# Exponentials and value products of four full attentions as a list of their own, and keys and queries in column halves

## The chip, the cores and the metric

The kernel runs on one core of one Trainium2 chip. The metric is device microseconds of one execution. The kernel before took 2460.37 us (median of 3 runs, 2451.26 to 2460.69).

## What is computed

`x` is [2, 1024, 256] in float32: two batches (b = 0, 1) of 1024 tokens. Four blocks follow each other, all with 16 heads of 16 channels where they attend.

```python
x = _L0(x)   # adaLN, window self-attention (128), top-16 cross-attention, SwiGLU MLP
x = _L1(x)   # prototype attention, three routed experts, gate
x = _L2(x)   # adaLN, masked full self-attention with rotary positions, cross-attention, GELU MLP
x = _L3(x)   # adaLN, full self-attention, cross-attention, GELU MLP

# the part that the change is about, in _L2 (with a mask) and in _L3 (without)
s = einsum('bqhd,bkhd->bhqk', q, k) * scale      # 1024 x 1024 scores per head
s = where(mask, s, finfo.min)                    # _L2 only
a = softmax(s, axis=-1)
o = einsum('bhqk,bkhd->bqhd', a, v)
```

## The kernel before

Work is written as *stages* (a norm, the keys of a batch, an attention, an MLP). A stage has one generator for each engine (`tensor`, `vector`, `scalar`, `pool`, `sync`); each `yield` ends a *step*, and a step is usually one instruction or one group of matmuls. The stages stand in *lists*: list 0 mostly holds the attentions, list 1 (its lane is `lane_d`) holds what runs beside them, the norms, projections, cross-attentions, MLPs and experts; a third list has loads for SyncE alone. For each engine, a string in `ORDER` says in which order the steps of the lists are issued: its characters are run lengths, in turn for list 0, list 1 and so on. The strings were written by a planner, ahead of time. Each engine works through its merged steps in order and waits on semaphores where it must.

A full attention (`Attention` with kind "full") treats 8 groups of 2 heads. For one group:

- SyncE loads the group's queries and keys, split in three bf16 parts each, from DRAM into a stack (`load`, L1072 and L1158). The stage `Begin` does that ahead for the first groups; the other loads are in the attention's own SyncE steps. The second block's attentions have two stacks, the last block's have three. A stack comes free after the last exponential of the group that had it.
- `max_tile` (L1224): 32 tiles of scores, 128 queries x 512 keys, into the banks 0 and 1. `max_of` (L1375 with the mask, L1378 without) takes each tile's row maxima on VectorE.
- The rows' maxima are joined (L1347), turned (L1193), split into two bf16 parts (`rows`, L1332 and L1335) and stored by SyncE into two rows of the query stack (L1171), so that the next matmul subtracts them.
- `exp_tile` (L1253): 32 tiles of transposed scores, 128 keys x 512 queries, into the banks 2 and 3. In the second block the mask is added, for half of the tiles by four small matmuls (L1258), for the other half ahead of the scores by ScalarE (L1318, `write_mask`). ScalarE takes the exponentials (L1300).
- `pv` (L1282): for every four tiles, the value products, four strips at once into bank 4. At the end of a group the sums are copied by ScalarE (`finish_copy`, L1080), turned (`finish_turn`, L1087), and divided by VectorE (`finish_out`, L1098 and L1104).

All of this was one stage in list 0, in beats: the exponentials of a group follow its maxima by 40 beats, with a period of 40 beats (second block) or 32 (last block), so that the exponentials of group g run with the maxima of group g + 1, one tile of each in turn. In the first 40 beats of an attention there are maxima alone, and in the last ones exponentials alone.

Keys and queries are made by `Parts` in four steps each, two column halves (channels 0 to 127 and 128 to 255) by two token blocks: matmuls (L854), ScalarE copies (L871, L877), VectorE splits (L926 and following), and three stores to DRAM by SyncE per step (L951), 12 for the keys and 12 for the queries of a batch. `PartsOf` does one column half of a `Parts`. The columns of half 0 hold the heads of groups 0 to 3. The function `halves` was already used for the first block and for the second block's batch 0:

```python
def halves(b, keys, queries, *begin):
    k, q = S_[b][keys], S_[b][queries]
    return [PartsOf(k, 0), PartsOf(q, 0), PartsOf(k, 1), *begin, PartsOf(q, 1)]
```

For the other three, the phase has keys, then queries, then values (`Values`, L999, L1021), then `Begin`. After the attention's outputs come the output projection (L1725, L1753, additions on VectorE at L1647) and the next norm (statistics at L719 and L724, turns at L767).

## Time and profile before

| | |
|---|---|
| median of 3 runs | 2460.37 us (2451.26 to 2460.69) |
| the profiled execution, its own time | 2454.07 us |
| its span in the profile | 2452.8 us |
| TensorE, VectorE, ScalarE busy | 92%, 69%, 57% |
| the four full attentions | 858 to 2250 us |

A profile shows one execution. Matmuls are pipelined: a matmul counts as busy from its start to its modelled end, so the times of neighbours overlap, and the starts show how fast TensorE goes. PE is TensorE's matmul, PEld its weight load, DVE VectorE, ACT ScalarE, POOL GpSimd, SP SyncE.

### The profile page before, as it was taken

The page shows a single profiled execution, that of the slowest core. Times are in us where ns is not written, and L with a number is a line of the kernel's source. Part 1 is how long each engine was busy: PE and PEld are TensorE (multiplying, and loading weights), DVE is VectorE, ACT ScalarE, POOL GpSimd, SP SyncE. Part 2 cuts the span into 40 slices and gives each one's busy share as a digit, 9 for nine tenths or more (in the row PEclk, how much of TensorE's full clock was granted, in tenths as well). Part 3 has the DMA queues.
Part 4 walks back from the last instruction along what each step waited for, and adds up shares of the span by engine and source line. Part 5 has one row for each costly group of instructions (what it writes and reads, how often), then busy time and mean ns, then how long its engine had stood idle before and what let it go on. Part 6 is the DMA issues. An engine that isn't in the chain of part 4 may idle for free.

```text
span 2452.8 us, 35316 instructions
## 1 busy us (share of the span) xinstructions
PE 2264.3 (92%) x12135; PEld 1146.1 (47%) x12135; DVE 1681.0 (69%) x5149; ACT 1407.8 (57%) x2698; POOL 371.9 (15%) x409
## 2 busy tenths in 40 slices
PE   7988799989998989998989999988999989999987
PEld 3675355645655644433343445443435342334554
DVE  7667876864325765677877776758786778885553
ACT  3434445543233236777848887855676747776543
POOL 3013533342201100000100010000020010002022
PEclk8998999998998979999989999988999999999999
DMA  7666521000001310001222200133130132210220
GB/s 232 167 180 193 159 79 33 14 22 5 14 1 47 121 16 14 23 18 53 99 87 67 60 23 14 47 113 99 46 79 14 52 97 85 62 40 7 61 65 18
DMA packets 151080, 161.06 MB, mean 66 GB/s; under 512 B 33423, under 2 KB 120291, under 8 KB 150637
## 3 DMA queue, kind: packets, MB, share of 16 engines
q1 hardware_dynamic: 150900, 158.80, 22.5%
q8 instruction: 96, 1.57, 0.3%
q14 instruction: 84, 0.68, 0.1%
HBM read 97.39 MB, written 60.19 MB: 64 GB/s over the span
## 4 chain that ended last, share of the span: by engine, by line
PE 73%; DVE 14%; ACT 6%; DMA 3%; issue 2%; POOL 2%; SPq 1%; ACTq 0%; DVEq 0%; POOLq 0%
PE bank L1282 10%; PE bank L1253 9%; PE bank L1833 9%; PE bank L1224 8%; PE bank L1856 6%; PE bank L2378 4%; PE bank L854 4%; PE bank L2558 3%; DVE max L1378 2%; PE bank L1753 2%; PE bank L1258 2%; ACT work L1300 2%; PE bank L2380 2%; PE bank L767 2%; PE bank L1087 2%
## 5 line engine op out<-in xcount | busy, mean ns | idle before, releaser
L1300 ACT ACTIVATE work<-bank 128x512 f32<-128x512 f32 (+1 forms) x1216 | 685.7, 595 | 271.5 <-PE bank L1253 173.4
L1375 DVE CUSTOM_DVE_ANT_0 bank<-bank,weights 128x512 f32<-128x512 f32 x512 | 347.8, 706 | 122.5 <-PE bank L1224 120.6
L1224 PE MATMUL bank<-k_stack,q_stack 97*128 97x512 bf16 x896 | 354.4, 401 | 34.2 <-DVE max L1378 15.5
L1378 DVE TENSOR_REDUCE max<-bank 128x1 f32<-128x512 f32 x512 | 334.5, 684 | 58.9 <-PE bank L1224 56.9
L1253 PE MATMUL bank<-q_stack,k_stack 99*128 99x512 bf16 x896 | 339.3, 384 | 21.5 <-ACT bank L1318 17.0
L1833 PE MATMUL bank<-hT,weights 128*128 128x512 f32 x512 | 254.2, 612 | 7.5 <-ACT hT L811 4.1
L1224 PEld LDWEIGHTS bank<-k_stack,q_stack 97*128 97x128 bf16 x896 | 88.5, 99 | 287.5 <-DVE max L1378 109.0
L1856 PE MATMUL bank<-weights,work 128*128 128x256 f32 x768 | 195.0, 383 | 4.2 <-DVE work L1923 3.8
L1856 PEld LDWEIGHTS bank<-weights,work 128*128 128x128 f32 x768 | 141.2, 190 | 67.9 <-issue 28.9
L1253 PEld LDWEIGHTS bank<-q_stack,k_stack 99*128 99x128 bf16 x896 | 86.7, 98 | 172.4 <-ACT work L1300 78.9
L1318 ACT ACTIVATE bank<-weights 128x512 f32<-128x512 uint8 x256 | 153.9, 602 | 6.9
L854 PE MATMUL bank<-hT,weights 128*128 128x512 f32 x288 | 150.8, 632 | 3.6 <-ACT hT L811 3.5
L1365 DVE TENSOR_REDUCE max<-bank 128x4 f32<-128x308 f32 (+1 forms) x192 | 101.8, 544 | 54.3 <-PE bank L1230 53.3
L1282 PE MATMUL bank<-work,v 128*17 128x512 f32 x1024 | 134.8, 598 | 0.0
L1282 PE MATMUL bank<-work,weights 128*17 128x512 f32 x1024 | 134.8, 598 | 0.0
L1833 PEld LDWEIGHTS bank<-hT,weights 128*128 128x128 f32 x512 | 93.7, 194 | 87.0 <-issue 60.1
L2378 PE MATMUL bank<-hT,weights 128*128 128x512 f32 (+1 forms) x240 | 123.3, 624 | 0.4 <-ACT work L2576 0.3
L1625 POOL TENSOR_TENSOR x<-x,row_consts 128x256 f32<-128x256 f32 x112 | 86.2, 770 | 189.1 <-DMA row_consts<-in_L_b_cproj 174.4
L2572 ACT ACTIVATE work<-bank,half_anchor 128x512 f32<-128x512 f32 x56 | 38.4, 686 | 113.2 <-PE bank L2380 106.3
L1258 PEld LDWEIGHTS bank<-ident_b,weights 128*128 128x128 bf16 x1024 | 79.0, 97 | 48.1 <-issue 0.3
L767 PE MATMUL bank<-ident,work 128*128 128x128 f32 x320 | 70.5, 339 | 31.7 <-DVE work L745 29.5
L1258 PE MATMUL bank<-ident_b,weights 128*128 128x128 bf16 x1024 | 99.1, 218 | 0.0
(236 smaller groups left out, 3669.8 us busy)
## 6 DMA issues: line engine op xcount, KB each, us to landing
q_stack<-parts_q SPq DMA_DIRECT2D x60, 384.0 KB, 4.0
k_stack<-parts_k SPq DMA_DIRECT2D x40, 384.0 KB, 5.0
parts_q<-parts SPq DMA_DIRECT2D x38, 384.0 KB, 2.5
weights<-parts_q SPq DMA_DIRECT2D x36, 384.0 KB, 3.6
parts_q<-parts SPq DMA_DIRECT2D x38, 256.0 KB, 2.9
parts_k<-parts SPq DMA_DIRECT2D x24, 384.0 KB, 2.6
parts_k<-parts SPq DMA_DIRECT2D x24, 256.0 KB, 2.9
weights<-in_L_e_w SPq DMA_DIRECT2D x12, 512.0 KB, 5.9
```

What stands on the lines that cost most here:

```text
L854: m = pe.e.matmul(bank.ap[:, :], w[:, i, self.col + c * P:self.col + (c + 1) * P], hT[self.b][:, bl, i, :], start=i == 0, stop=i == CC - 1)
L1224: m = pe.e.matmul(bank.ap[:, :], self.q(g)[0:MAX_ROW, h, qt * P:(qt + 1) * P], k_stacks[self.key, g].ap[0:MAX_ROW, h, half * BLK:(half + 1 ...
L1253: m = pe.e.matmul(bank.ap[0:self.nk, :], self.k(g, h, STACK, kt * P), q, start=not written, stop=written or not self.mask, skip_group_chec ...
L1258: m = pe.e.matmul(bank.ap[:, j * P:(j + 1) * P], mask_bias[:, half * TPB + j, kt * P:(kt + 1) * P], ident_b[:, :], start=False, stop=j == ...
L1282: m = pe.e.matmul(o[strip:strip + DV, :], self.v[:, kt, head, :] if self.own else self.v[:, head, :], p[0:self.nk, :], start=kt == 0, stop ...
L1300: ac.e.activation(p.ap[0:self.nk, :], banks[self.key, "exp", g, i].ap[0:self.nk, :], ACT.Exp).then_inc(*probs.tick((self.key, g, i)))
L1318: ac.e.activation(bank.ap[:, :], masked_of[self.b][:, i // 4, :], ACT.Copy, scale=MASKED).then_inc(*evac.tick((self.key, "masked", g, i)))
L1375: ve.e.tensor_tensor_reduce(bank[:, :], bank[:, :], mask_bias[:, qt, half * BLK:(half + 1) * BLK], 1.0, -3.4e38, ALU.add, ALU.max, to).the ...
L1378: ve.e.tensor_reduce(to, bank[:, :], AX_X, ALU.max).then_inc(*maxima.tick((self.key, g, i)))
L1833: m = pe.e.matmul(banks[key].ap[:, :], w1[:, k, col:col + P], hT[self.b][:, bl, k, :], start=k == 0, stop=k == CC - 1)
L1856: m = pe.e.matmul(banks[self.key, tp].ap[:, i * C:(i + 1) * C], hid[:, at * P:(at + 1) * P], w2[:, j, :], start=(j == 0 and i == 0), stop= ...
L2378: return pe.e.matmul(out, wt[name][:, k, lo:hi], hT[self.b][:, self.bl, k, :], start=k == 0, stop=False)
```

## The change

1. `Attention` of kind "full" becomes `FullAttention`, whose steps on TensorE and VectorE are the maxima and what belongs to them; on ScalarE it has none. A new stage `Weighting` has the exponentials, masks written by ScalarE, value products, and the finish of a group. The four `Weighting` stages stand in a list of their own. The beats without an instruction are no longer steps.
2. The merge of TensorE, VectorE and ScalarE goes over three lists.
3. Keys and queries of the second block's batch 1 and of the last block's both batches are made by `halves`, with `Begin` for one group (before: two, two and three groups, behind the values).
4. All order strings are new, over the whole kernel.

```diff
@@ ORDER: every string of the five engines is replaced; the first line of two of them
     "tensor": (
-        "1932342d1e3a912142328142c45222c222h2c132l142f2o2222e315bb343724341Mal2c272636432227212927273eb56526961ea622442234181"
+        "1903202403r0490910220420720430420220a20540120d20610d10310g10j20h20na0860580960630330650610Oa0h10510c2021021071022024"
     "scalar": (
-        "0Zdi6b629hb714221B521bl6bZakd755272696DbUk2126948321835451Zl5kfa4b8b838i7113898o8gg1171c112a12c3bc4a24172529le757a63"
...
@@ Attention.scalar
-                        g, i = now
-                        p = work[self.key, "prob", g, i]
...
+                        yield from self.exponentials(ac, *now)
+            def exponentials(self, ac, g, i):
+                p = work[self.key, "prob", g, i]
+                if self.mask and (g, i) == (0, 0):
+                    for first in range(2):
+                        self.write_mask(ac, 0, first)
+                        yield
+                for f in p.free:
+                    ac.wait_ge(*f)
+                ac.wait_ge(*exp_scores[self.key, g, i])
+                ac.e.activation(p.ap[0:self.nk, :], banks[self.key, "exp", g, i].ap[0:self.nk, :], ACT.Exp).then_inc(
+                    *probs.tick((self.key, g, i)))
+                yield
...
@@ new stages
+        class FullAttention(Attention):
+            def tensor(self, pe):
+                turns = 0
+                for beat in range(self.beats):
+                    if now := self.group(beat, 0, self.n):
+                        self.max_tile(pe, *now, turns)
+                        yield
+                        turns += 1
+                    if now := self.group(beat, self.rows_at + 1, 1):
...
+                        pe.e.transpose(bank.ap[0:PAIR * NT, 0:P], max1[self.key, g].ap[:, :], ident[:, :]).then_inc(
+                            *turned.tick((self.key, "rows", g)))
+                        yield
+                        turns += 1
+            def scalar(self, ac):
+                return iter(())
+            def vector(self, ve):
+                for beat in range(self.beats):
+                    if now := self.group(beat, self.rows_at + 2, 1):
+                        yield from self.rows_of(ve, now[0])
+                    if now := self.group(beat, 0, self.n):
+                        self.max_of(ve, *now)
+                        yield
+                    if now := self.group(beat, self.rows_at, 1):
+                        self.both_halves(ve, now[0])
+                        yield
+        class Weighting(Stage):
+            def __init__(self, attn):
+                self.attn = attn
+            def tensor(self, pe):
+                attn = self.attn
+                for beat in range(attn.beats):
+                    if now := attn.group(beat, attn.exp_at, attn.n):
+                        attn.exp_tile(pe, *now)
+                        yield
+                    if now := attn.group(beat, attn.pv_at, attn.n):
+                        if now[1] % 4 == 0:
+                            attn.pv(pe, now[0], now[1] // 4)
+                            yield
+                    if now := attn.group(beat, attn.fin_at + attn.late, 1):
+                        g = now[0]
+                        bank = banks.take(attn.bank("pv", g), (attn.key, "turn", g), (vec, (attn.key, "out", g)))
+                        attn.finish_turn(pe, g, bank)
+                        yield
+            def scalar(self, ac):
+                attn = self.attn
+                for beat in range(attn.beats):
+                    if now := attn.group(beat, attn.exp_at, attn.n):
+                        yield from attn.exponentials(ac, *now)
+                    if now := attn.group(beat, attn.fin_at, 1):
+                        attn.finish_copy(ac, now[0])
+                        yield
+            def vector(self, ve):
+                attn = self.attn
+                for g in range(attn.groups):
+                    yield from attn.finish_out(ve, g)
@@ build_program
-            st["self2"] = Attention(lane_a, b, "L2", "full", ...
+            st["self2"] = FullAttention(lane_a, b, "L2", "full", ...
-            st["self3"] = Attention(lane_a, b, "L3", "full", ...
+            st["self3"] = FullAttention(lane_a, b, "L3", "full", ...
-        begin_win1, begin_self1 = Begin(two_["win"]), Begin(two_["self2"])
-        begin_last, begin_last1 = Begin(one_["self3"], 2), Begin(two_["self3"])
+        begin_win1, begin_self1 = Begin(two_["win"]), Begin(two_["self2"], 1)
+        begin_last, begin_last1 = Begin(one_["self3"], 1), Begin(two_["self3"], 1)
-            (of(0, "self2"), of(1, ("e", 1, "n"), ("e", 1)) + [v_high2, mask_copy] + of(1, "n4", "k2", "q2", "v2") + [early(0, "so2"), begin_self1],
-             [Rest(30), load_l2m, load_l3]),
+            (of(0, "self2"), of(1, ("e", 1, "n"), ("e", 1)) + [v_high2, mask_copy] + of(1, "n4") + halves(1, "k2", "q2", begin_self1) + of(1, "v2") + [early(0, "so2")],
+             [Rest(30), load_l2m, load_l3], [Weighting(one_["self2"])]),
...
-             + of(0, "mlp2", "n7", "k3", "q3") + [early(0, "v3")] + of(0, "v3") + [early(1, "so2"), begin_last]),
+             + of(0, "mlp2", "n7") + halves(0, "k3", "q3", begin_last) + [early(0, "v3")] + of(0, "v3") + [early(1, "so2")], [], [Weighting(two_["self2"])]),
...
-            merge(ORDER["tensor"], *[itertools.chain.from_iterable(s.tensor(pe) for s in lane) for lane in lanes[0:2]])
+            merge(ORDER["tensor"], *[itertools.chain.from_iterable(s.tensor(pe) for s in lane) for lane in (lanes[0], lanes[1], lanes[3])])
```

The turn of a finished group now takes the bank of the value products (4) in place of one of the two maxima banks.

## Rows read from the trace of the kernel before

**Rows 1.** The page: its span, and busy time of each engine.
```profile
span 2452.8 us, 35316 instructions
...
PE 2264.3 (92%) x12135; PEld 1146.1 (47%) x12135; DVE 1681.0 (69%) x5149; ACT 1407.8 (57%) x2698; POOL 371.9 (15%) x409
```

**Rows 2.** The page's costliest groups: busy us, mean ns, idle before.
```profile
L1300 ACT ACTIVATE work<-bank 128x512 f32<-128x512 f32 (+1 forms) x1216 | 685.7, 595 | 271.5 <-PE bank L1253 173.4
L1375 DVE CUSTOM_DVE_ANT_0 bank<-bank,weights 128x512 f32<-128x512 f32 x512 | 347.8, 706 | 122.5 <-PE bank L1224 120.6
L1224 PE MATMUL bank<-k_stack,q_stack 97*128 97x512 bf16 x896 | 354.4, 401 | 34.2 <-DVE max L1378 15.5
L1378 DVE TENSOR_REDUCE max<-bank 128x1 f32<-128x512 f32 x512 | 334.5, 684 | 58.9 <-PE bank L1224 56.9
L1253 PE MATMUL bank<-q_stack,k_stack 99*128 99x512 bf16 x896 | 339.3, 384 | 21.5 <-ACT bank L1318 17.0
...
L1318 ACT ACTIVATE bank<-weights 128x512 f32<-128x512 uint8 x256 | 153.9, 602 | 6.9
```

**Rows 3.** Timeline of TensorE in the last attention: start us, duration us.
```profile
2131.11 0.39 PE L1224 MATMUL bank<-weights 97*128 97x512 bf16 x1
2131.33 0.38 PE L1253 MATMUL bank<-q_stack,k_stack 99*128 99x512 bf16 x1
```

**Rows 4.** Busy time by stage: length, each engine's busy us, granted clock, DMA.
```profile
0.00:858.00 858.00, 766.05 (x3882) 472.46 (x3883) 557.61 (x2414) 345.56 (x809) 238.47 (x264) 0.94 0.31 90
...
908.00:1230.00 322.00, 303.70 (x1802) 130.23 (x1800) 224.17 (x617) 247.39 (x431) 17.47 (x13) 1.00 0.14 41
1230.00:1272.00 42.00, 33.42 (x142) 18.18 (x140) 30.71 (x94) 12.45 (x23) 5.08 (x5) 0.84 0.24 62
1272.00:1618.00 346.00, 336.96 (x2132) 154.99 (x2132) 245.02 (x694) 287.02 (x512) 17.31 (x18) 1.00 0.20 58
1618.00:1682.00 64.00, 52.40 (x185) 23.81 (x185) 49.47 (x101) 19.38 (x34) 6.02 (x6) 0.76 0.32 96
1682.00:1978.00 296.00, 292.59 (x1579) 122.28 (x1579) 218.07 (x455) 206.82 (x377) 22.07 (x25) 1.00 0.22 59
1978.00:2020.00 42.00, 34.68 (x146) 19.17 (x145) 36.80 (x82) 11.62 (x21) 9.72 (x12) 0.92 0.21 55
2020.00:2250.00 230.00, 224.95 (x1349) 76.05 (x1347) 183.59 (x370) 170.07 (x315) 12.88 (x17) 1.00 0.18 52
```

**Rows 5.** Timeline of TensorE where the second attention begins.
```profile
1234.92 1.03 PE L999 MATMUL bank<-weights,hT 128*128 128x256 f32 x4
1238.07 0.59 PE L1224 MATMUL bank<-k_stack,q_stack 97*128 97x512 bf16 x2 [2.12 <-DMA k_stack<-parts_k]
...
1252.14 0.60 PE L1224 MATMUL bank<-k_stack,q_stack 97*128 97x512 bf16 x2
1257.17 1.26 PE L1224 MATMUL bank<-k_stack,q_stack 97*128 97x512 bf16 x2 [4.44 <-DVE max L1375]
```

**Rows 6.** Timeline of VectorE in that pause.
```profile
1252.94 0.75 DVE L719 BATCH_NORM_STATS2 stats<-x 128x6 f32<-128x256 f32 x2
...
1255.53 0.72 DVE L719 BATCH_NORM_STATS2 stats<-x 128x6 f32<-128x256 f32 x2
```

**Rows 7.** Timeline of SyncE's DMA issues ahead of the second attention.
```profile
1216.29 13.05 SPq L951 DMA_DIRECT2D parts_q<-parts  x9
...
1230.59 0.49 SPq L1158 DMA_DIRECT2D k_stack<-parts_k  x1
```

**Rows 8.** What weight loads waited for, 858 to 2250 us: total, times, longest.
```profile
PEld bank L1224 <- DVE max L1378: 135.7, 242, 4.7
PEld bank L1224 <- DVE max L1375: 105.7, 152, 4.9
PEld bank L1253 <- ACT work L1300: 90.6, 192, 1.0
...
PEld bank L1253 <- ACT bank L1318: 55.7, 101, 1.0
```

**Rows 9.** Timeline of TensorE where the fourth attention begins.
```profile
1984.42 0.59 PE L1224 MATMUL bank<-k_stack,q_stack 97*128 97x512 bf16 x2 [0.50 <-DMA k_stack<-parts_k]
```

More of the change, by code:

```diff
@@ L1309, in scalar @@
                         yield
+                    yield
[11 more added lines that the diff above has]
+                yield
+                n = g * self.n + i + 2
+                if self.mask and n < self.groups * self.n and self.head_half(n % self.n)[1] == 0:
+                    self.write_mask(ac, n // self.n, n % self.n)
                     yield
@@ L1339, in vector, with rows_of, both_halves @@
                         yield
[L1340 to L1350 removed]
+                    yield
+            def rows_of(self, ve, g):
+                mp = max_parts.take(self.in_a, (self.key, g), (ld_m[self.q_lane(g)], (self.key, g)))
+                for f in mp.free:
+                    ve.wait_ge(*f)
+                ve.wait_ge(*turned[self.key, "rows", g])
+                src = banks[self.key, "rows", g].ap[0:PAIR * NT, 0:P]
+                ve.e.tensor_copy(mp.ap[:, 0, :], src).then_inc(*vec.tick((self.key, "high", g)))
+                yield
+                ve.wait_ge(*vec[self.key, "high", g])
+                ve.e.tensor_tensor(mp.ap[:, 1, :], src, mp.ap[:, 0, :], ALU.subtract).then_inc(*vec.tick((self.key, "rows", g)))
+                yield
+            def both_halves(self, ve, g):
+                m1 = max1.take(g % 2 + 2 * self.in_a, (self.key, g), (turned, (self.key, "rows", g)))
+                for f in m1.free:
+                    ve.wait_ge(*f)
+                ve.wait_ge(*maxima[self.key, g, self.n - 1])
+                ve.e.tensor_reduce(m1.ap[:, :], max2[self.key, g].ap[:, :, :], AX_X, ALU.max).then_inc(
+                    *maxima.tick((self.key, g, "rows")))
             def max_of(self, ve, g, i):
@@ L1378, in max_of @@
                     ve.e.tensor_reduce(to, bank[:, :], AX_X, ALU.max).then_inc(*maxima.tick((self.key, g, i)))
+        class FullAttention(Attention):
[8 more added lines that the diff above has]
+                        g = now[0]
+                        bank = banks.take(self.bank("max", turns), (self.key, "rows", g), (vec, (self.key, "rows", g)))
+                        for f in bank.free:
+                            pe.wait_ge(*f)
+                        pe.wait_ge(*maxima[self.key, g, "rows"])
+                        pe.e.transpose(bank.ap[0:PAIR * NT, 0:P], max1[self.key, g].ap[:, :], ident[:, :]).then_inc(
[7 more added lines that the diff above has]
+                    if now := self.group(beat, self.rows_at + 2, 1):
+                        yield from self.rows_of(ve, now[0])
+                    if now := self.group(beat, 0, self.n):
[4 more added lines that the diff above has]
+                        yield
@@ L2860, in build_program @@
             k_rows = [("k_rows2", 0), ("k_rows2", 1)]
[L2861 removed]
+            st["self2"] = FullAttention(lane_a, b, "L2", "full", st["q2"], st["k2"], (V, V_high)[b], [(vec, (st["v2"].key, "all"))],
                                     [(dense, (st["v2"].key, "all"))], rows_ready=k_rows, keys_ready=[],
```

153 lines of the change are left out of this document (77 added, 76 removed).

## The prediction

> **What bounds the kernel now.** I read the page first: over the 2452.8 us span TensorE is busy for 92%, VectorE for 69%, ScalarE for 57% [rows 1]. So TensorE is the engine to watch, but a busy TensorE is not one at its peak, and an average hides where it stands. The costliest groups [rows 2] belong to the four full attentions (the second and the third block's self-attentions, two batches each): an exponential takes 0.60 us, a maximum 0.71 us with the mask and 0.68 us without, a mask written by ScalarE 0.60 us. The matmuls beside them show 0.40 and 0.38 us, but they are pipelined: a maxima matmul begins at 2131.11 and the exponentials' matmul behind it at 2131.33, so a tile costs TensorE 0.22 us where nothing is waited for [rows 3].
>
> Next I read the busy time by stage, cut at the change from one attention to the next [rows 4]. The stretches between are the four interiors (908 to 1230, 1272 to 1618, 1682 to 1978, 2020 to 2250 us). TensorE idles in them for 18.3, 9.0, 3.4 and 5.1 us, 35.8 us in all, at a full granted clock. The three later transitions (1230 to 1272, 1618 to 1682, 1978 to 2020) are 148 us long and idle for 8.6, 11.6 and 7.3 us, 27.5 us in all; their granted clock is 0.84, 0.76 and 0.92, which is 42 x 0.16 + 64 x 0.24 + 42 x 0.08 = 25 us of full clock. There ScalarE is nearly empty (12.5 of 42 us in the first) while VectorE works 30.7 of 42: the old attention has run out of exponentials, and the new one has only maxima. The part before the attentions idles for 92 us in 858.
>
> The timeline shows what ends the pauses at a transition [rows 5]. The first maxima matmul of the second attention begins at 1238.07 after 2.12 us for its keys' transfer. At 1257.17 another waited 4.44 us for a maximum: VectorE had gone to the next list's additions and eight statistics of a norm, 1252.94 onward [rows 6]. SyncE explains the transfer: the last nine stores of queries take 13.05 us of its issue, and the keys' load is issued only at 1230.59 [rows 7]. The waits of the weight loads, last, say what holds attention tiles in general: banks that VectorE and ScalarE have yet to free, 241 us and 146 us in sum [rows 8]. Most of that lies under matmuls still running, so it is no idle time to be had back.
>
> **The change, part by part.** No instruction is added or removed in number but a few no-op steps of the lists; what is moved is which list an instruction belongs to, and the order in which five engines issue. I read both order strings by the kernel's own rule (runs of steps, one list after the other).
>
> *The third list alone* allows exponentials and value products to be placed free of the maxima. What the strings do with it is less than could be done. At the transitions the new attention's maxima still start almost where they did. On TensorE, before the second attention, three maxima tiles now stand ahead of the last value product of the old one (none did); before the third, its first maximum stands some two steps earlier; before the fourth, two stand ahead. The head of 32 maxima with no exponential beside it stays, and so does VectorE's block of statistics: the 4.4 us pause is not touched.
>
> *The halves.* Keys and queries now go out as keys half 0, queries half 0, keys half 1, queries half 1, and the load of group 0 follows the third of these rather than the fourth. That is six stores fewer ahead of it: 6 x 13.05 / 9 = 8.7 us earlier by [rows 7], so issue near 1221.9, and with the 7.5 us from issue (1230.59) to the waiting matmul (1238.07) it lands near 1229.4. No matmul is added: both halves were separate matmuls before. Only the group 0 load is early; groups 1 and 2 are issued by SyncE at the attention's own first step, behind the old one's last exponentials, which they need for their buffers anyway; with 32 maxima in between they are covered.
>
> The transition terms, then: before the second attention 3 x 0.70 = 2.1 us of maxima leave the head that VectorE bounds, and the 2.12 us wait goes: 4 us at most. The first maximum now stands ahead of the last four exponentials, that is near 1227.5 in the old time, so if the load lands at 1229.4, TensorE stands with those exponentials queued behind it, and ScalarE with them: some 2 us come back. I take 3, between 2 and 4. Before the third: one maximum, 0.7 us. Before the fourth: 2 x 0.68 and the wait of 0.50 us [rows 9], 1.9 us. Sum 5.6, taken as 6 us. The norm's block and the next list's products hide none of this; if the cover of the old exponentials is gone, the term is 0.
>
> *The interiors.* The strings alternated strictly before, one maximum, one exponential. In the new ones 230 maxima tiles follow a maximum directly (68 before) and 194 exponentials follow one (63 before), with everything else of the other list within a few places of where it was. The exception is the first attention: its first two groups run beside some 20 fewer steps of the experts' products, which are handed to groups 2 and 3. What this gives has no row. Bounds: 0, and the 35.8 us that TensorE idles there. The nearest row is the next attention: if 908 to 1230, with 5.7% idle, came to the 2.6% of 1272 to 1618, it would be 322 x 0.031 = 10 us. I take 10. A loss is not excluded, and is the rival below.
>
> *The first 858 us* get a new order too though the change has no reason there; the same steps shift by a few places. I take 0, with bounds of plus and minus a tenth of the 92 us idle, 9 us.
>
> Sum: 6 + 10 = 16 us off the profiled execution, 2454.1 us (its span of 2452.8 and 1.3 around it). The three runs have a median of 2460.4 and go from 2451.3 to 2460.7; the profiled one lies within them, 6 us under the median. A saving of 16 us from the median gives 2444 us.
>
> **A rule weighed.** In an interior TensorE makes short waits for banks all the time and its granted clock stays at 1.00; it fell only where TensorE had stood for 4 us [rows 4, 5]. The Trainium skill, "TensorE: Matmul & The Clock Gate", section "A second HAM failure mode: psum-queue depth-cycling", says that a kernel which cycles through accumulator banks can make TensorE pause between groups so often that its clock swings between its two levels. By that rule pairs on two banks would be a risk; the trace so far disagrees.
>
> **Rivals.**
> *Pairs cost more than they save (slower).* In a pair, the second tile needs the other bank free too. If VectorE is just on it, TensorE stands 0.70 - 0.22 = 0.48 us; for exponentials 0.60 - 0.22 = 0.38 us. There are 162 more pairs of maxima and 131 of exponentials: 162 x 0.48 + 131 x 0.38 = 128 us if every one were exposed. From one in eight exposed (16 us) the forecast gain is gone; from 28 us, a bit over one in five, the kernel is slower by 0.5%. At one in four it costs 32 us: 2460 - 16 + 32 = 2476 us. For it: the waits of [rows 8]. Against: a pair is followed by a pair of the other kind, so each bank has as long as before on average. Chance 0.16.
> *It does little.* The head stays bound by VectorE, a maximum made early is waited for at the same statistics block, and what is saved in an interior is returned at the next join, the lists being in step at nearly the same places. Time 2455 to 2460. For it: the new attention starts with the same neighbours. Against: the interior idle time is there to be had. Chance 0.30.
> *The freedom pays in full.* The interior 36 us and the 6 us, and half of the 25 us of clock at the joins because the pauses shrink: 55 us, 2405 us. Against: the 4.4 us pause stays. Chance 0.10.
> *The clock falls in the interiors.* If one attention of 370 us ran at 0.85 as a mean, it would cost 55 us: 2444 + 55 = 2499, on the slow side. It is what the rule of the Trainium skill above would do here. Chance 0.02.
> *The forecast:* 2444, its own range 2434 to 2453. Chance 0.42.
>
> **Numbers.** Change from no change can be told here by about 0.5%, 12 us. Faster: 0.42 + 0.10 = 0.52. Same: 0.30. Slower: 0.16 + 0.02 = 0.18. The range from 2414 to 2474 leaves out a little over half of the slow cases and the far part of the large gain.
>
> **What would show it.** The load of group 0's keys issued about 9 us before the last query store ends, and no wait for it over 0.5 us; three maxima ahead of the last value product at the first of the three joins; the 4.4 us pause there as before; idle TensorE from the first attention's start to its end down by about 10 us, with the other interiors nearly unchanged; a clock of 1.00 in all four. The prediction is wrong if waits for banks grow in number and length, if TensorE stands for keys with exponentials behind it, or if the first 858 us move by more than 9 us.

## The result, and the profile after

The changed kernel took 2423.8 us (median of 4 runs, 2417.4 to 2428.6) beside 2460.2 us for the kernel before (4 runs): a ratio of 0.9865, interval 0.9845 to 0.9886, so 28 to 38 us less. A second set gave 0.9885 (0.9867 to 0.9904). Single executions that took 8% or more longer at a lower granted clock, one of the kernel before among them, are left out of all times. Faster was right, and the time lies in the wide range given (2414 to 2474), but below the forecast's own (2434 to 2453): 16 us less was forecast, less than half of what came.

The page of the kernel after, against [rows 1, 2]:

```profile
span 2416.1 us, 35295 instructions
...
PE 2237.6 (93%) x12135; PEld 1141.8 (47%) x12135; DVE 1667.4 (69%) x5149; ACT 1404.6 (58%) x2698; POOL 370.8 (15%) x409
...
L1338 ACT ACTIVATE work<-bank 128x512 f32<-128x512 f32 (+1 forms) x1216 | 682.8, 594 | 251.7 <-PE bank L1285 162.7
...
L1256 PE MATMUL bank<-k_stack,q_stack 97*128 97x512 bf16 x896 | 325.2, 391 | 33.4 <-DVE max L1409 18.0
L1285 PE MATMUL bank<-q_stack,k_stack 99*128 99x512 bf16 x896 | 326.1, 384 | 10.6 <-DMA q_stack<-max_parts 2.8
```

Counts are those of before, durations too but for the maxima's matmul (401 ns, now 391); what has moved is waits. Ahead of the exponentials' matmuls (L1285, before L1253) TensorE idles for 10.6 us instead of 21.5, and the mask that ScalarE writes, once their chief reason with 17.0 us, is no longer it. By stage, cut at the same steps as [rows 4] (the first line is the time ahead of the attentions; 899, 1252, 1657 and 1988 begin the interiors):

```profile
0.00:852.00 852.00, 761.15 (x3884) 470.49 (x3885) 546.80 (x2414) 346.74 (x809) 237.54 (x264) 0.95 0.31 91
899.00:1204.00 305.00, 294.88 (x1759) 130.84 (x1758) 214.25 (x605) 238.09 (x418) 16.20 (x12) 1.00 0.14 44
1204.00:1252.00 48.00, 37.75 (x186) 19.68 (x185) 38.40 (x109) 20.52 (x36) 6.85 (x6) 0.93 0.23 64
1252.00:1596.00 344.00, 335.23 (x2124) 155.27 (x2122) 242.83 (x692) 284.32 (x511) 17.30 (x18) 1.00 0.20 60
1596.00:1657.00 61.00, 49.60 (x224) 22.80 (x221) 50.28 (x106) 23.52 (x42) 6.01 (x6) 0.92 0.31 91
1657.00:1938.00 281.00, 277.54 (x1499) 117.97 (x1497) 215.13 (x447) 195.43 (x357) 22.22 (x25) 1.00 0.21 53
1938.00:1988.00 50.00, 43.04 (x195) 23.07 (x194) 39.54 (x84) 20.17 (x37) 9.71 (x12) 0.93 0.30 87
1988.00:2217.00 229.00, 225.27 (x1356) 77.00 (x1355) 185.22 (x374) 169.62 (x315) 13.98 (x19) 1.00 0.18 51
```

The clock rounds to 1.00 in all four interiors, as before, and is 0.93, 0.92, 0.93 in the three joins (0.84, 0.76, 0.92 in before, over windows of 42, 64 and 42 us where these are 48, 61 and 50).

SyncE's issues ahead of the second attention, against [rows 7], TensorE's timeline there, against [rows 5], and what weight loads waited for between 850 and 2220 us, against [rows 8]:

```profile
1194.11 7.31 SPq L983 DMA_DIRECT2D parts_k<-parts  x6
...
1202.17 0.47 SPq L1190 DMA_DIRECT2D k_stack<-parts_k  x1
1205.61 7.29 SPq L983 DMA_DIRECT2D parts_q<-parts  x6
```

```profile
1207.86 0.38 PE L1256 MATMUL bank<-k_stack,q_stack 97*128 97x512 bf16 x1 [0.78 <-DMA k_stack<-parts_k]
...
1213.17 0.38 PE L1256 MATMUL bank<-k_stack,q_stack 97*128 97x512 bf16 x1
...
1216.37 1.05 PE L1314 MATMUL bank<-work,v 128*17 128x512 f32 x8
...
1237.11 1.26 PE L1256 MATMUL bank<-k_stack,q_stack 97*128 97x512 bf16 x2 [4.37 <-DVE max L1409]
```

```profile
PEld bank L1285 <- ACT work L1338: 192.5, 340, 1.0
PEld bank L1256 <- DVE max L1412: 86.9, 164, 4.9
PEld bank L1256 <- DVE max L1409: 74.1, 136, 4.7
...
PEld bank L1285 <- ACT bank L1352: 30.0, 83, 1.2
```

The load of group 0's keys is issued at 1202.17, 10.7 us ahead of the end of the last query stores; TensorE still waits 0.78 us for it (2.12 before); the statistics block still costs 4.37 us. Two maxima (1207.86 and 1213.17) stand ahead of the last value product at 1216.37. The weight loads wait less for maxima (161 us for 241) and for the mask (30.0 for 55.7), and far more for ScalarE's exponentials (192.5 for 90.6), most of it under matmuls that still run.

**A sharper instrument.** A profile's idle time counts from the modelled end of a matmul. I took starts instead: from one TensorE start to the next, less the pace at which such an instruction goes where nothing is waited for (0.22 us for an attention tile, [rows 3]; 0.43 us for a 512-column float32 matmul, two of which stand 0.86 us apart in the timelines; 0.99 us for a group of eight value products; the others in proportion to their columns). What is left is a *gap*; half-speed clock falls into it too. Span less all gaps is 2024.8 us for before and 2024.2 for after, and between 2023.9 and 2026.1 in every other run. It can't be much else: it is the count of instructions times their paces, and the counts are equal. So the gaps, 428.0 us and 392.0, are a way to say where the difference lies, and no proof of its cause. How they split by kind hangs on the paces taken, by 1 to 3 us a stretch and up to 5 in A2.

The table goes by the start of VectorE's maxima. A1 to A4 reach from an attention's first maximum (A1), its group 1's (A2, A4) or group 2's (A3) to its group 7's; J1 to J3 are what lies between. "After" is the mean over the profiled runs that issue after's order in that stretch (three are left out, see below); "half clock" is the time in which TensorE was granted 0.50, in before, then in the single runs of after's order; the last three columns are gaps of before and after (second run), ahead of a maximum's matmul, ahead of an exponential's, and ahead of all others.

| stretch | before, us | after, us | difference | half clock, us | maxima | exponentials | others |
|---|---|---|---|---|---|---|---|
| up to A1 | 860.9 (mean of 4) | 857.8 (mean of 9) | -3.1 | | | | |
| A1 | 305.1 | 294.7 | -10.4 | 30.7; 20.5 | 13.9, 16.8 | 15.8, 6.8 | 25.1, 21.2 |
| J1 | 109.2 | 105.6 | -3.6 | 13.7; 6.8 to 13.7 | 13.0, 11.6 | 8.4, 2.5 | 6.9, 10.3 |
| A2 | 269.3 | 268.4 | -0.9 | 0; 0 or 3.4 | 2.8, 3.9 | 10.4, 9.8 | 12.4, 11.7 |
| J2 | 158.9 | 151.9 | -7.0 | 30.7; 6.8 to 20.5 | 19.0, 16.3 | 6.0, 4.4 | 13.7, 12.4 |
| A3 | 206.7 | 200.3 | -6.4 | 0; 0 | 3.6, 0.8 | 0.9, 3.0 | 8.2, 7.9 |
| J3 | 105.5 | 107.2 | +1.7 | 6.8; 6.8 to 10.2 | 12.3, 9.4 | 0.6, 1.4 | 6.0, 5.1 |
| A4 | 175.5 | 174.8 | -0.7 | 0; 0 | 6.9, 3.2 | 1.4, 4.5 | 8.2, 6.3 |
| after A4 | 264.1 | 263.2 | -0.9 | | | | |

The stretches add up to 31 us less. Some of them need care.

- *The first maximum.* That it stands at 851.8 us in after's first profile was luck: nine runs with that order have it between 851.8 and 862.7.
- *Runs left out.* front_before has after's order in A1 and takes 298.1 us; att1_before has it in A2 and A4 and takes 271.6 and 179.2. Each was at half clock there for 6.8 us more than after_again was. With them the differences are -10.0, -0.4 and -0.1.
- *A1 by groups.* Group 0's maxima, which have no exponentials beside them, take 50.6 us in before (30.7 of them at half clock) and 47.7 in after (20.5); group 1's take 55.0 and 44.6; those of groups 3 and 4 take 3 us more each in after. At the paces above, list 1's matmuls in group 1 fell from 28 to 17 us, and in groups 3 and 4 they rose by 4 and 6: 9.5 us of work came in for 6 us of time. So the 2.9 us of group 0 go with the clock, and the rest goes with where list 1's work stands as well as with the order of the tiles. No run parts these two; alternate keeps list 1's work in its place and still loses 13.0 us in A1.
- *A3.* Of its 6.4 us, 5 are work that has moved to J3 (at the paces above, 194 us of matmuls became 189 in A3, 87 became 91 in J3).
- *J2 goes with the clock.* The rows are before, after, after_again and joins23_before (the last two are told below); the third number from the end is the granted clock:

```profile
1541.90:1700.80 158.90, 144.27 (x749) 63.83 (x751) 112.67 (x261) 99.27 (x178) 10.48 (x10) 0.90 0.27 84
1521.90:1673.50 151.60, 137.84 (x758) 62.07 (x757) 111.80 (x265) 100.79 (x180) 10.46 (x10) 0.97 0.30 90
1531.10:1685.90 154.80, 142.75 (x758) 64.13 (x757) 112.23 (x265) 100.59 (x180) 10.46 (x10) 0.93 0.28 88
1523.50:1681.80 158.30, 144.54 (x751) 64.62 (x753) 112.99 (x263) 99.43 (x178) 10.46 (x10) 0.90 0.27 85
```

The same program had 10.2 us at half clock and J2 in 151.5 us one time, 20.5 and 154.8 the other; three more runs of its order had 6.8 and 151.0 to 151.2. before and joins23_before had 30.7. All of them make the pause of 4.36 or 4.37 us for the statistics; a second one of 2.15 us for a maximum, 33 us behind it, stands in those last two alone. From 6.8 to 20.5 us at half clock costs 3.7 us, so 24 us more would cost 6.5 (an estimate from these runs): most of J2's 7.

### The profile page after: what moved, and what is told of

The parts are those of the page before. It is cut to its first block, busy times and chain, and to the rows that moved or that the text cites. A ratio compares the mean times of both kernels' runs of the same rounds, so it can differ in the third digit from the quotient of the medians.

```text
span 2416.1 us, 35295 instructions
## 1 busy us (share of the span) xinstructions
PE 2237.6 (93%) x12135; PEld 1141.8 (47%) x12135; DVE 1667.4 (69%) x5149; ACT 1404.6 (58%) x2698; POOL 370.8 (15%) x409
## 3 DMA queue, kind: packets, MB, share of 16 engines
q1 hardware_dynamic: 150900, 158.80, 22.6%
## 4 chain that ended last, share of the span: by engine, by line
PE 74%; DVE 13%; ACT 4%; DMA 3%; POOL 2%; issue 2%; SPq 1%; DVEq 0%; ACTq 0%; POOLq 0%
PE bank L1314 11%; PE bank L1285 10%; PE bank L1938 9%; PE bank L1256 8%; PE bank L1961 7%; PE bank L2483 4%; PE bank L886 3%; PE bank L2663 3%; PE bank L1858 3%; PE bank L1290 2%; PE bank L2485 2%; DVE bank L1409 2%; PE bank L799 2%; PE bank L1119 2%; ACT work L1338 1%
## 5 line engine op out<-in xcount | busy, mean ns | idle before, releaser
L1256 PE MATMUL bank<-k_stack,q_stack 97*128 97x512 bf16 x896 | 325.2, 391 | 33.4 <-DVE max L1409 18.0
L1285 PE MATMUL bank<-q_stack,k_stack 99*128 99x512 bf16 x896 | 326.1, 384 | 10.6 <-DMA q_stack<-max_parts 2.8
L1938 PE MATMUL bank<-hT,weights 128*128 128x512 f32 x512 | 255.4, 610 | 5.5 <-ACT hT L843 2.5
L1285 PEld LDWEIGHTS bank<-q_stack,k_stack 99*128 99x128 bf16 x896 | 85.6, 97 | 241.2 <-ACT work L1338 165.1
L886 PE MATMUL bank<-hT,weights 128*128 128x512 f32 x288 | 143.0, 601 | 2.9 <-ACT hT L843 2.8
L1399 DVE TENSOR_REDUCE max<-bank 128x4 f32<-128x308 f32 (+1 forms) x192 | 101.6, 543 | 48.7 <-PE bank L1262 47.7
```

Source lines behind the costliest of these rows:

```text
L886: m = pe.e.matmul(bank.ap[:, :], w[:, i, self.col + c * P:self.col + (c + 1) * P], hT[self.b][:, bl, i, :], start=i == 0, stop=i == CC - 1)
L1256: m = pe.e.matmul(bank.ap[:, :], self.q(g)[0:MAX_ROW, h, qt * P:(qt + 1) * P], k_stacks[self.key, g].ap[0:MAX_ROW, h, half * BLK:(half + 1 ...
L1285: m = pe.e.matmul(bank.ap[0:self.nk, :], self.k(g, h, STACK, kt * P), q, start=not written, stop=written or not self.mask, skip_group_chec ...
L1938: m = pe.e.matmul(banks[key].ap[:, :], w1[:, k, col:col + P], hT[self.b][:, bl, k, :], start=k == 0, stop=k == CC - 1)
```

## The experiments

The order strings of all kernels here are made by splicing those of before and after step by step. In pairs_on_before and mask_order_on_before, which put before's order through the new three lists, VectorE, ScalarE and GpSimd issue exactly the instructions of before in before's order, and TensorE too wherever it was not edited: **the third list alone changes nothing**. And the change had an edit that the prediction passed over, though the diff shows it: the turned sums (`finish_turn`) go to the `pv` bank 4 and no longer take one of the two maxima banks in turn. After's order isn't free of deadlock with the turns in the old banks, nor is before's with them in the new one, so bank and order are changed together below, and each of these splices tests both at once. The helper line is

```diff
-                        bank = banks.take(attn.bank("pv", g), (attn.key, "turn", g), (vec, (attn.key, "out", g)))
+                        ahead = f"{attn.name}{attn.b}{g}" in TURN_AHEAD
+                        bank = banks.take(attn.bank("max", attn.turns) if ahead else attn.bank("pv", g), (attn.key, "turn", g), (vec, (attn.key, "out", g)))
+                        attn.turns += ahead
```

Ratios are to the kernel before, run beside each; after's two are 0.9865 and 0.9885, mean 0.9875. 0.001 of a ratio is 2.5 us, and an interval reaches some 5 us to either side, that of a difference between two kernels some 6. The times in place, from the table's stretches, are finer.

### after_again

The kernel after, unchanged.

> The kernel after, unchanged, as a measure of chance: att1_before and after issue the same order ahead of the first attention, and yet their first maxima came 9.0 us apart (860.8 and 851.8 us). If the 851.8 us of after's profile was luck, this run shows the first maximum near 858 to 861, with its span up by as much, and the stretches inside the attentions unchanged within 3 us; if it is the order's doing, it comes at 852 again. The time by ratio: 0.985 to 0.989 of before.

0.9885 (0.9867 to 0.9904). First maximum at 862.7 us: luck, as expected. From there on it keeps after's times within 0.2 us up to group 3 of attention 2, within 2 us to the last attention's last group, and is 3.8 us behind at the end; J2 took 3.2 us more and A2 1.8 less. One cause of both is seen: the clock stood at half 10.2 us longer in J2, and for 3.4 us in after's A2 but not here.

### front_before

```diff
 ORDER of all five engines
-    after's steps up to the first full attention
+    before's steps up to the first full attention
```

> The kernel after, with the order of the kernel before on every engine up to the start of the first full attention; from there on the order of after. Theory: the 6.5 us by which the first attention's first maximum comes earlier in after are earned by the new order ahead of it and carried to the end unchanged, so this kernel takes 6.5 us more than after (about 2430) and every later step of it lies as far behind after's. Rival (the front's gain is absorbed in the attentions, whose VectorE or ScalarE would have waited anyway): under 2 us more than after. Rival (the difference of the two profiled executions was chance): the first maximum at the same time as in after.

0.9897 (0.9875 to 0.9918), some 5 us more than after, with an interval that holds 0. First maximum at 861.8, within after's own spread. Means of 860.9 and 857.8 us over four and nine runs (858.4 to 862.5, and 851.8 to 862.7) put the front at about 3 us, not clear of that spread; the forecast of 6.5 rested on one lucky profile.

### att1_before

```diff
+TURN_AHEAD = ('L200', 'L201', 'L202', 'L203', 'L204', 'L205', 'L206')
 ORDER of tensor, vector, scalar, in attention 1 (L2, batch 0)
-    after's steps from its first maximum to group 7's exponentials
+    before's
```

> The kernel after, with the order of the kernel before from the first maximum of attention 1 to group 7's exponentials of it (its turns of hT back in maxima banks). Theory: the 10.2 us between the first maximum and group 7's in after come from the order inside this attention, through fewer waits of TensorE for ScalarE's mask scores (before 12.0 us in 25 waits between 900 and 1250 us): this kernel takes 8 to 11 us more than after, the waits for the mask are back at about 12 us in this attention, and the later attentions are as in after. Rival (the time comes from elements of the first attention that lane 1's other work, not the order of its matmuls, lengthens, and is made up again behind it): under 3 us more than after.

0.9929 (0.9906 to 0.9951), 13 us more than after. In place: A1 302.1 us, 7.4 more, and J1 1.6 more, so 9.0 of the 8 to 11. Waits for the mask are back: 10.4 us in 20 up to 1250 us. The gaps say it fully: ahead of exponentials 15.7 us in A1 (before 15.8, after 6.8), ahead of maxima 12.8 (13.9, 16.8). The order gives 9 us on the one side and pays 4 on the other. Not as expected, the later attentions moved too, on after's order: A2 3.2 us more, A4 4.4. In each TensorE stood once for the transfer of a group's maxima (1.7 and 1.95 us) and was at half clock for 6.8 us, from about then on; the same pause in A2 was 1.24 us in after and 0.84 in after_again. So a part of the 13 us is not attention 1's.

### att3_before and att3_before_2

```diff
+TURN_AHEAD = ('L301', 'L302', 'L303', 'L304', 'L305')
 ORDER of tensor, vector, scalar, in attention 3 (L3, batch 0), groups 2 to 7
-    after's steps
+    before's
```

> The kernel after, with the order of the kernel before in groups 2 to 7 of attention 3 only (its turns of hT in maxima banks). Theory: the 6 us by which that stretch was shorter in after than in before (from 27.4 to 33.4 us ahead) are the order's: this kernel takes 5 to 8 us more than after. Rival (they are chance or come from the join ahead of it): within 2 us of after.

> The same kernel as att3_before, once more for a profile that can be read by stage. Theory: the stretch from group 2's first maximum of attention 3 to group 7's is 5 to 8 us longer than in after (200.8 us there), and nothing else moves. Rival (something further on answers to it): the stretch within 2 us of after's, with more lost behind it.

0.9923 and 0.9929, 12 and 13 us more than after. In the second one's profile A3 is 210.6 us, 10.3 more, of which 2.5 come back in J3: 7.8 in place. 5 us of A3's is matmul work that before's order has there and after's in J3; of the rest 3.4 us are one wait for a maximum, behind VectorE's other work, and 3.4 us at half clock follow it, which is 1.7 us lost. Bank and order aren't parted here: turn_bank, below, loses 6.3 us in A3 by the bank alone.

### joins23_before

```diff
+TURN_AHEAD = ('L217', 'L300', 'L306', 'L307', 'L310')
 ORDER of tensor, vector, scalar, from group 7 of an attention to group 2 of the next, joins 2 and 3
-    after's steps
+    before's (the column halves stay)
```

> The kernel after, with the order of the kernel before around the second and third of the three joins, from group 7's maxima of one attention to group 2's of the next; the column halves stay. Theory: the two joins gave 5.0 and -1.8 us, so this kernel takes 2 to 5 us more than after. Rival (the new order at the joins gives nothing by itself, what was gained there came from the halves): within 2 us of after. Either way the granted clock at the joins stays about what it is.

0.9930 (0.9909 to 0.9952), 13 us more than after; in place J2 158.3 us (6.4 more; before 158.9) and J3 108.4 (1.2 more). So what J2 gave comes from the order (with the bank of five turns in these stretches), and the halves, which stay here, give nothing there. My 2 to 5 us were too low, and the clock did not stay what it was: in J2 it was at half for 30.7 us, as in before, where after's order has 6.8 to 20.5.

### turn_bank

```diff
+TURN_AHEAD = ('L205', 'L206', 'L207', 'L211', 'L213', 'L216', 'L217', 'L301', 'L302', 'L303', 'L305', 'L306', 'L307', 'L310', 'L316', 'L317')
```

> The kernel after, its order unchanged, with the turned sums (hT) of 16 of the 32 groups put back from their bank 4 into a maxima bank. Theory (the bank is only what makes the order possible): within 3 us of after. Rival (a turn in a maxima bank makes the next maxima wait for VectorE's division, 8.4 us in 11 waits in before, none in after): 3 to 6 us slower than after.

0.9912 (0.9891 to 0.9933), 9 us more; in place 6.3 in A3, 2.0 in J1 (of which some goes with 13.7 us at half clock there; front_before, with as much, had 0.7) and 1.4 in A4. The rival is right in kind, though it costs more than its 3 to 6 us, and half of A3's comes in a way that neither theory named. TensorE's timeline in group 3 of attention 3, then its windows (the last three numbers are clock, DMA share, GB/s):

```profile
1723.28 1.05 PE L1315 MATMUL bank<-work,v 128*17 128x512 f32 x8
...
1731.93 0.39 PE L1257 MATMUL bank<-k_stack,q_stack 97*128 97x512 bf16 x1 [1.50 <-DVE hT L1137]
...
1735.41 1.93 PE L1315 MATMUL bank<-work,v 128*17 128x512 f32 x8
```

```profile
1730.00:1733.00 3.00, 1.50 (x11) 0.64 (x10) 1.73 (x5) 1.03 (x2) 0.00 (x0) 0.94 0.00 0
1733.00:1737.00 4.00, 4.00 (x19) 0.58 (x17) 1.75 (x4) 1.73 (x4) 0.00 (x0) 0.50 0.02 4
1737.00:1741.00 4.00, 4.00 (x18) 1.86 (x14) 1.57 (x3) 2.13 (x4) 0.00 (x0) 0.69 0.95 255
1741.00:1745.00 4.00, 3.94 (x23) 1.10 (x26) 3.51 (x8) 2.98 (x7) 1.27 (x1) 1.00 0.13 40
```

A maximum's matmul stands 1.50 us for the division of the turned sums, and then the clock is at half: the group of value products takes 1.93 us for 1.05. That is 4 x 0.50 + 4 x 0.31 = 3.2 us of full clock lost.

### pairs_on_before

One place of the order on TensorE, before and after the edit (M a maximum, E an exponential of the group before, o a step of list 1):

```diff
-M12 E12 o M13 E13 M14 E14 pv2 M15 E15 M16 E16 o M17 E17 M18 E18 pv3 M19 E19
+E12 M12 o M13 E13 E14 M14 pv2 M15 E15 E16 M16 o M17 E17 E18 M18 pv3 M19 E19
```

> The order of the kernel before on every engine, with no column halves for the later keys and queries and the turns of hT in maxima banks; only on TensorE, inside the four full attentions, are maxima and exponentials put in pairs (two maxima, then two exponentials). Of neighbours of one kind there are 223, 223, 215 and 215 in the four, against 46 to 68 of each kind over all four in before. Theory A (the pairing is what shortens the interiors, since two matmuls of a kind give ScalarE and VectorE time to clear both banks of the other): 15 to 20 us less than before (2440 to 2445), the interiors of attentions 1 and 3 down by 8 to 10 us each. Theory B (the pairing is a by-product; what counts is where the other steps, mask scores above all, lie between the maxima): within 5 us of before. Rival C (pairs fill a kind's banks and make the second matmul wait): 5 us or more above before, with the waits of TensorE for VectorE's maxima longer.

1.0159 (1.0134 to 1.0183): 39 us **slower** than before, all four attentions: A1 13.1 us more, A2 10.7, A3 7.5, A4 5.5. The rival C is right as to the time; the times of theories A and B did not come. But the growth is mostly ahead of exponentials (A1 25.7 us of gaps for 15.8), less ahead of maxima (16.3 for 13.9).

### alternate

```diff
-E12 M7 M8 o M9 o o E13 M10 M11 E14 pv2 E15 M12 M13 E16 o o E17 M14 M15 E18 pv3 E19 M16 M17 E20
+M8 E12 o M9 o o E13 M10 E14 M11 pv2 E15 M12 E16 M13 o o E17 M14 E18 M15 pv3 E19 M16 E20
```

> The kernel after, with maxima and exponentials of attentions 1, 2 and 4 on TensorE put in turn wherever no other step stands between them (neighbours of one kind 153, 151 and 111 down to 36, 32 and 18); all else as in after. pairs_on_before was 38 us slower than before, so pairs by themselves cost. Theory (pairs are a by-product, what counts is where the steps stand against VectorE's and ScalarE's order): this kernel is slower than after too, by 5 to 20 us, since TensorE's order no longer fits that of the other two. Rival (pairs cost in after as well, and the gain comes from elsewhere): 5 to 15 us faster than after.

0.9997 (0.9983 to 1.0010): 30 us slower than after, more than I gave it, and the whole gain is gone, though VectorE, ScalarE, banks and halves are after's. In place: A1 13.0, J1 4.0, A2 5.8, J2 4.0, A4 3.9. (J2 says little: it had 20.5 us at half clock, as after_again had, which took 154.8 us to this one's 155.9.) In A1 the gaps ahead of exponentials are 22.6 us (after 6.8) and those ahead of maxima 12.4 (16.8). Waits of TensorE from 850 us on, those for the mask first:

```profile
PE bank L1287 <- ACT bank L1354: 15.3, 34, 0.7
PE bank L1258 <- DVE max L1411: 14.6, 19, 4.4
PE bank L1258 <- DVE max L1414: 13.7, 15, 4.4
```

### mask_order_on_before

After's string shows a pattern: of its exponentials in attentions 1 and 2, those of tiles 2 and 3 of each four, which need no mask from ScalarE, follow another exponential twice as often (145 times, other steps between them left out of account) as those of tiles 0 and 1, which do (74). This kernel gives before that pattern and nothing else.

```diff
-M0 E0 M1 E1 M2 E2 M3 E3
+M0 M1 E0 M2 E1 E2 M3 E3
```

> The order of the kernel before on every engine (no column halves for the later keys and queries, turns in maxima banks), but for one thing: in attentions 1 and 2, of each four tiles on TensorE the maximum between the second and the third exponential goes ahead of the first one (M E0 M E1 M E2 M E3 becomes M M E0 M E1 E2 M E3; 56 places in each). The first two of each four need a mask that ScalarE writes into their bank, the last two do not. Theory D (what the new order gives in attentions 1 and 2 is that TensorE comes later to the tiles that wait for ScalarE's mask and goes through the others together: the waits for it were 17.0 us in 38 in before, 16.3 in pairs_on_before, 15.3 in alternate and 2.6 in after): the waits fall to under 6 us and the kernel is 10 to 15 us faster than before. Rival (one place in four moved alone does not fit VectorE's order, and the waits for maxima grow as in pairs_on_before): the waits for the mask fall but the time is within 5 us of before, or above it.

1.0170 (1.0147 to 1.0193): 42 us slower than before. The same view as above:

```profile
PE bank L1259 <- DVE max L1412: 33.3, 97, 4.4
PE bank L1259 <- DVE max L1415: 15.8, 15, 4.4
PE bank L1288 <- ACT work L1341: 13.7, 46, 0.5
...
PE bank L1288 <- ACT bank L1355: 2.4, 7, 0.6
```

The waits for the mask fell to 2.4 us in 7 (after's 2.6 in 7, before's 17.0 in 38), and 97 waits for a masked maximum came in their place, 17 before. In A1 the gaps ahead of maxima are 30.7 us for 13.9. Theory D is refuted as a sufficient cause. It also shows how local this is: A3 and A4, whose order is untouched, take 206.9 and 175.2 us (before 206.7 and 175.5).

### pairs_on_after

```diff
-E12 M7 M8 o M9 o o E13 M10 M11 E14 pv2 E15 M12 M13 E16 o o E17 M14 M15 E18 pv3 E19 M16 M17 E20
+E12 o M9 o o M10 E13 E14 M11 pv2 M12 E15 E16 M13 o o M14 E17 E18 M15 pv3 M16 E19 E20
```

> The kernel after, with maxima and exponentials of attentions 1, 2 and 4 on TensorE re-sequenced into pairs (two maxima, two exponentials) wherever no other step stands between them; VectorE's and ScalarE's order, the banks and the halves as in after. Directly neighbouring maxima in these three attentions: 243 against after's 173; exponentials 309 against 140. mask_order_on_before had as many direct neighbours in attentions 1 and 2 as after has (124 maxima and 134 exponentials; after 130 and 89) and was 40 us slower than before. Theory (a pair pays or costs by the place where it stands; made by rule, pairs cost on any base): 10 to 40 us slower than after, and no attention quicker. Rival (pairs by rule cost only where VectorE and ScalarE keep the order of before): within 5 us of after, or faster.

1.0136 (1.0114 to 1.0157): 64 us slower than after, well beyond my 10 to 40; attention 3, not edited, keeps its 200.2 us. In A1 the gaps ahead of exponentials are 26.2 us (after 6.8), in A2 20.6 (9.8); the clock stays at 1.00 from 905 us to the end of A1, and in A2, A3 and A4.

### stats_spread

```diff
 VectorE's order at the first join (the same at the other two)
-norm statistics 0 to 18, M16 M17 M18
+norm statistics 0 to 4, M16, 5 to 9, M17, 10 to 14, M18, 15 to 18
```

> The kernel after, with VectorE's order alone changed at the three joins: the norm's statistics that stand in one block there (TensorE waits 4.4 us for a maximum behind them) are interleaved with three or four maxima. Theory: the 4.4 us waits fall under 2 us, TensorE's granted clock does not drop there, and the kernel is 5 to 12 us faster than after. Rival (the norm and the projections behind it end later, and the join is bound by them): within 3 us of after or slower, the wait turned from maxima to the norm's turn.

0.9916 (0.9892 to 0.9939), 10 us more than after; in place J1 3.2 us more, J2 0.8, J3 1.1. Waits of TensorE for maxima, the longest last (after: 4.4 and 4.4 us; their sums in the second run 18.1 and 13.2):

```profile
PE bank L1256 <- DVE max L1409: 20.7, 34, 3.6
PE bank L1256 <- DVE max L1412: 15.7, 18, 2.1
```

The one long pause became several, and their sum grew (31.3 us to 36.4). At the first join one of them is still 3.6 us, and the clock still fell: 13.7 us at half in J1, 10.2 in J2. Spreading what causes the pause didn't cut it away. That VectorE is the bound of a join fits this, and isn't shown by it; nor was the later norm, the expectation's rival, looked at by itself.

## Why the prediction was right or wrong

- **Transitions, forecast -6: measured -8.9** (J1 -3.6, J2 -7.0, J3 +1.7). The first join gave the 3 us, but only in part as worked out: two maxima stand ahead of the last value product and not three, the key's wait fell by 1.3 us and not 2.1 (0.78 us was left where I had said at most 0.5), and the gaps that shrank are mostly those ahead of exponentials (8.4 to 2.5 us). The second join was put at one maximum, 0.7 us, and gave 7: **this term failed**. joins23_before shows that it is the order, and the clock is how most of it comes (30.7 us at half speed, 6.8 to 20.5 with the new order, without the second pause of 2.15 us). The sum had nothing for the clock at the joins, though the prediction had priced it at 25 us, because the 4.4 us pause would stay. It stayed, and the clock was back sooner. The third join was to give 1.9 us and cost 1.7, since work moved there.
- **Interiors, forecast -10: measured -18.4** (A1 -10.4, A2 -0.9, A3 -6.4, A4 -0.7). This is the step that failed most: "What this gives has no row ... I take 10." The first attention gave just that, 2.9 us of it ahead of the interior that I had measured (from 908 us on), the rest mostly in group 1, through fewer waits ahead of exponentials. That the size fits is in part luck. The third was given nothing, since the page shows it nearly without idle time (3.4 us). Part of its 6.4 us is work moved to J3; A3 and J3 together gave 4.7. With the runs that the table leaves out, the interiors gave 16.9.
- **The bound of 35.8 us was no bound.** It was idle time behind modelled ends. By starts, TensorE's gaps in A1 to A4 of before are 54.8, 25.6, 12.7 and 16.5 us, 110 in all.
- **The turn's bank was not costed at all.** It carries some 8 us: turn_bank puts 16 of 32 turns back, and loses 6.3 in A3 and 2.0 in J1. That before lost its A3 time in this way is not shown; its trace has no such wait there.
- **The first 858 us, forecast 0: about -3,** within what one profile can't tell.
- **Where the clock falls.** The prediction read that it fell only where TensorE had stood for 4 us. Before's granted clock was 0.50 from 1239.1 to 1242.4, right behind the wait of 2.12 us [rows 5]. The runs show falls behind shorter pauses still (last section).
- **The rival "pairs cost more than they save"** names a real price. Pairs set by rule cost 39 us on before's order and 64 on after's. What I had wrong there is which side pays: mostly the exponentials. That after's own order has 230 and 194 such neighbours and is faster shows that the count doesn't decide.
- **The reason, as far as shown.** It is the order, with the bank that allows it: put back in place by splices on all three engines, before's order takes back 9.0 us in A1 and J1, 7.8 in A3 and J3, and 7.6 in J2 and J3, 24 of the 31. That the order of maxima and exponentials on TensorE must be just after's is shown by alternate, where nothing else differs and the whole gain is gone. But the four kernels made by rule change TensorE alone, against orders of VectorE and ScalarE made for another, so their losses may be the misfit's and don't price the pairs. It isn't the number of pairs (mask_order_on_before has 124 maxima and 134 exponentials directly behind one of their kind in attentions 1 and 2, after 130 and 89) nor the waits for the mask alone (that kernel has none left to speak of). Each rule tried moved waits from one pair of banks to the other, or made more. What makes a given place good, the state of VectorE and ScalarE when TensorE comes to it or the neighbours from list 1, is argued, not isolated. Nor was before's order at the first join tried with the halves kept, so what the halves give there is open.

## What to carry to other kernels

Where TensorE feeds two engines through two banks each, the order in which it serves them is worth some per cent in either direction, and none of three simple rules (alternate, pair, late to the slow one), laid over TensorE's order alone, found it: each lost 30 us or more here. Judge such an order by TensorE's gaps from start to start, split by what stands behind the gap, before and after; busy shares hide two thirds of them. Look at the granted clock of each stretch too, in more than one execution, before a few microseconds are put down to the order. And look through a diff for edits it doesn't announce: one changed bank was worth a quarter of this gain.

## What the hardware showed unexpectedly

- **Half speed after short pauses, but not each time.** In turn_bank TensorE stood for 0.24 and then 1.50 us between 1729 and 1732 us, in a stretch otherwise full, and its clock was 0.50 from 1733 to 1737. Past the first attention's first 50 us there are nine such falls inside the attentions, in seven of the runs, each of 3.4 or 6.8 us, and each near a pause of 0.87 to 3.35 us. The pause alone doesn't decide. alternate and pairs_on_after both stand for 2.18 us, at 1041.89 and 1042.34, for the same transfer; the first is at half clock from 1043.07 on for 3.4 us, the second stays at 1.00. The Trainium skill, "TensorE: Matmul & The Clock Gate", section "A second HAM failure mode: psum-queue depth-cycling", tells of a kernel whose small pauses between groups came so often that its clock swung. Here many small pauses did no such thing: mask_order_on_before has 129 idle times of 0.15 to 1 us in those stretches, the most of the runs counted, and not one fall.
- **The same program repeats to 0.1 us in one stretch and not in the next.** Two executions of after differ by 10.9 us at the first maximum, by 0.1 us over the next 295 (A1), and by 3.2 us in J2. Runs with the same order on the three engines range over 293.7 to 298.1 us in A1 and 174.2 to 179.2 in A4, the longest being those with more time at half clock. One profile prices an edit to a microsecond only where the clock is the same.
